# Queries, keys and values projected by three float32r products of parts, by halves of the rows

## The chip, the cores and the metric

The kernel runs on one core of one Trainium2 chip. The metric is the device time of one execution in microseconds; each given time is that of the whole program. Five engines work side by side, each with its own instruction stream in program order: TensorE (PE in the profile; PEld is its weight load), VectorE (DVE), ScalarE (ACT), GpSimd (POOL) and SyncE (SP, which here only starts transfers). They wait for one another on semaphores.

## The reference, cut to what matters

```python
x = x + attn(layernorm(x), qkv_w, qkv_b, out_w, out_b)            # x: (4, 1024, 256)
x = x + xattn(layernorm(x), ctx_1024, ...)                         # context: (4, 77, 256)
x = x + ffn(layernorm(x), W_router, b_router, W1, b1, W2, b2)      # 8 experts, top 2
# attn:
qkv = x @ qkv_w.T + qkv_b                                          # 256 -> 768, all rows
qkv = qkv.reshape(batch, seq_len, 16, 48).transpose(0, 2, 1, 3)
q, k, v = jnp.split(qkv, 3, axis=-1)                               # 16 heads of 16
scores = jnp.einsum('bhid,bhjd->bhij', q, k) / 4 + alibi_bias
out = jnp.einsum('bhij,bhjd->bhid', softmax(scores), v)
```

All is float32. The change touches the first product, from 256 features to the queries, keys and values of 1024 rows, once for each of four batches.

## The kernel before, in words

The program has three stages. In the **opening** (0 to about 90 us) batch 0 is normalized, turned and projected, and the row maxima of its first group of heads are taken. In the **attention stage** (to about 1085 us) 16 groups run, four for each batch, each of four heads. A group has 64 units; a unit is one score product of 128 keys by 512 queries (`score`, L1110), its exponential on ScalarE (`exp`, L1360), a quarter of an `attend` (L1124, products with the values), and, for a later group, one product for row maxima (`max`, L1150) with its reduction on VectorE (`maxed`, L1539; in the first group L1536 reduces two at once). In the **expert stage** (to the end) 71 blocks of 128 rows pass through the experts.

What sets the order is `plan()`. It writes one list of steps and each engine runs its own kinds of step in the order of the list. Beside the units it places side work in two lanes. The lane "next" prepares batch b+1 during batch b (`prepare`); the lane "done" completes batch b-1. `behind()` gives each lane a budget per unit (`PACE_NEXT`, `PACE_DONE`), and the number behind each `yield` is what a step takes of it. `TAKES` holds the planner's costs, by which `until()` and `room()` hold a step back until its input or its PSUM bank should be ready.

`prepare(b)` before: `layer_norm` (statistics L1579, `norm` L1378 from `xr_next` into `xn_next`), four `turn`s (L1171, four 128x128 transposes each into one of two side banks) with their copies `turned` (L1386) into `xT_next`, which holds all 1024 rows. Then 8 projections `proj` per batch: `mo` is the half of the 256 output features, `a` is queries or keys, `ch` is the half of the rows. Each is two float32 products of 512 columns (L1180), one per half `c` of the input features, and each of these two is a part of its own in the order. A projection is split into three bfloat16 parts: `high` on ScalarE (L1394), `rest` on VectorE (L1610, from PSUM into one of two buffers `rest_of`), and `mid` and `low` (L1511, L1514) on GpSimd, in the first half of batch 0 on VectorE. Last come 4 `vproj` per batch (L1189), each of two parts of two float32 products of 256 columns, and `values` (L1623) reads the result.

The parts of the queries and keys are written to DRAM (`stage`, L1013; for the first half of batch 0 `first_half`, L998 on SP, L1402 on ACT) and read back in stacked form (`spread`, L987, L988; for the first group L1001 on SP and L1352 on ACT). The first `max` waits for the stacked rows of the first group (`first_rows`).

An fp32 product is issued as two instructions in the trace, so 4 batches x 8 x 2 products are the 128 instructions of L1180.

## Time and profile before

| | us |
|---|---|
| median of 3 runs | 1623.58 |
| lowest and highest | 1622.12, 1631.59 |
| the profiled execution, its own time | 1623.51 |
| its span in the profile | 1621.7 |

```profile
PE 1563.1 (96%) x10430; PEld 952.5 (59%) x10430; DVE 1180.4 (73%) x2393; ACT 936.4 (58%) x1788; POOL 392.2 (24%) x463
PE   5999999999999999999999999989999999999996
DVE  4887877878777788886777777523444788888885
PE 89%; DVE 4%; ACT 3%; issue 2%; DMA 1%; POOL 0%; ACTq 0%; DVEq 0%; SPq 0%; POOLq 0%
```

The first line has each engine's busy time, its share of the span and its instructions. The next two show the busy share in 40 slices of 40.5 us, in tenths. The last is the chain of waits that ended last: at each step from the last instruction back, which engine the time belongs to. Matmuls overlap in the records, so a busy PE is not PE at its peak: what a product costs is read from the distance between starts, not from its duration.

### The profile page before, as it was taken

How to read it: one execution, taken by the hardware profiler on the slowest of the kernel's cores; microseconds unless marked ns; L12 is line 12 of the kernel's file. 1: busy time of each engine (PE TensorE's matmuls, PEld its weight loads, DVE VectorE, ACT ScalarE, POOL GpSimd, SP SyncE). 2: the span in 40 equal slices, each digit the busy share in tenths (PEclk: the TensorE clock that was granted, in tenths of full speed). 3: DMA queues.
4: the chain of work that ended last, by engine and by line, in shares of the span. 5: the costliest groups of instructions: out<-in, count | busy, mean ns of one | idle time of the engine just before them, and what ended most of it. 6: DMA issues, size and time to landing. Idle time of an engine off the chain costs nothing.

```text
span 1621.7 us, 30987 instructions
## 1 busy us (share of the span) xinstructions
PE 1563.1 (96%) x10430; PEld 952.5 (59%) x10430; DVE 1180.4 (73%) x2393; ACT 936.4 (58%) x1788; POOL 392.2 (24%) x463
## 2 busy tenths in 40 slices
PE   5999999999999999999999999989999999999996
PEld 2433343343444444345444344438999999999996
DVE  4887877878777788886777777523444788888885
ACT  3156656666555766754665755872222566666663
POOL 6201120001210041310013100051243433453443
PEclk9899999999999999999999999999999999999998
DMA  6663341133141440314234333134566776666663
GB/s 177 111 125 58 78 82 23 22 44 56 36 61 65 69 74 23 43 40 82 51 65 76 36 113 131 62 127 143 144 192 190 194 200 215 201 197 196 195 191 85
DMA packets 92670, 173.40 MB, mean 107 GB/s; under 512 B 13235, under 2 KB 51123, under 8 KB 92384
## 3 DMA queue, kind: packets, MB, share of 16 engines
q1 hardware_dynamic: 75376, 143.69, 35.1%
q0 software_dynamic: 15744, 26.54, 7.7%
q8 instruction: 84, 1.38, 0.4%
q10 hardware_dynamic: 1392, 1.18, 0.4%
q14 instruction: 74, 0.61, 0.1%
HBM read 133.69 MB, written 37.29 MB: 105 GB/s over the span
## 4 chain that ended last, share of the span: by engine, by line
PE 89%; DVE 4%; ACT 3%; issue 2%; DMA 1%; POOL 0%; ACTq 0%; DVEq 0%; SPq 0%; POOLq 0%
PE ps L1316 15%; PE ps L1124 15%; PE ps L1150 14%; PE ps L1110 13%; PE ps L1079 8%; PE ps L1342 4%; PE ps L1180 3%; PE ps L1202 2%; PE ps L1171 2%; PE ps L1236 2%; PE ps L1113 2%; PE ps L1153 2%; DVE rmax L1539 2%; ACT prob L1360 2%; PE ps L1189 2%
## 5 line engine op out<-in xcount | busy, mean ns | idle before, releaser
L1539 DVE TENSOR_REDUCE rmax<-ps 128x1 f32<-128x512 f32 x960 | 622.5, 684 | 187.6 <-PE ps L1150 91.2
L1360 ACT ACTIVATE prob<-ps 128x512 f32<-128x512 f32 x1024 | 559.6, 605 | 316.2 <-PE ps L1113 165.6
L1150 PE MATMUL ps<-stacked_k,stacked_q 112*128 112x512 bf16 x1024 | 389.7, 387 | 11.2 <-DMA stacked_k<-parts_of_rows 3.4
L1110 PE MATMUL ps<-stacked_q,stacked_k 115*128 115x512 bf16 x1024 | 357.4, 381 | 4.8 <-ACT prob L1360 3.2
L1124 PE MATMUL ps<-prob,values 128*32 128x512 f32 x2048 | 272.8, 605 | 5.8 <-ACT prob L1360 5.3
L1316 PE MATMUL ps<-xiT,w_now 128*128 128x128 f32 x2272 | 267.7, 276 | 1.0 <-issue 1.0
L1316 PEld LDWEIGHTS ps<-xiT,w_now 128*128 128x128 f32 x2272 | 262.5, 193 | 2.0 <-issue 1.2
L1150 PEld LDWEIGHTS ps<-stacked_k,stacked_q 112*128 112x128 bf16 x1024 | 99.1, 98 | 279.5 <-DVE rmax L1539 183.4
L1110 PEld LDWEIGHTS ps<-stacked_q,stacked_k 115*128 115x128 bf16 x1024 | 98.0, 98 | 160.5 <-ACT prob L1360 79.1
L1939 POOL DMA_INDIRECT out<-yo,xi x71 | 116.5, 1640 | 247.8 <-DVE yo L1827 240.9
L1466 ACT ACTIVATE hidT<-ps,b 128x128 f32<-128x128 f32 x284 | 80.1, 364 | 87.8 <-PE ps L1316 77.8
L1813 DVE TENSOR_TENSOR w_low<-w,w_high 128x2048 fp32r<-128x2048 f32 x51 | 116.9, 2293 | 5.5 <-issue 4.0
L1476 ACT ACTIVATE hid_high<-hidT 128x512 fp32r<-128x512 f32 x102 | 64.6, 633 | 94.3 <-DVE hidT L1796 92.6
L1079 PE MATMUL ps<-w_high,hid_high 128*128 128x256 f32 x408 | 118.7, 291 | 0.0
L1796 DVE TENSOR_SCALAR hidT<-ps,b 128x128 f32<-128x128 f32 x284 | 80.1, 344 | 47.5 <-PE ps L1316 37.9
L1079 PE MATMUL ps<-w_low,hid_high 128*128 128x256 f32 x408 | 114.6, 281 | 0.0
L1079 PE MATMUL ps<-w_high,hid_low 128*128 128x256 f32 x408 | 114.6, 281 | 0.0
L1153 PE MATMUL ps<-ramps,slopes 128*128 128x128 f16 x512 | 112.7, 220 | 0.0
L1113 PE MATMUL ps<-ramps,slopes 128*128 128x128 f16 x512 | 112.3, 219 | 0.0
L1853 POOL TENSOR_TENSOR rstd_of<-varp,minus_half 128x8 f32<-128x8 f32 (+1 forms) x14 | 20.8, 1485 | 362.9 <-DVE varp L1587 362.9
L1488 ACT ACTIVATE w_high<-w 128x2048 fp32r x51 | 97.6, 1913 | 17.7 <-issue 16.0
L1805 DVE TENSOR_TENSOR hid_low<-hidT,hid_high 128x512 fp32r<-128x512 f32 x102 | 70.2, 688 | 45.5 <-ACT hid_high L1476 45.5
(201 smaller groups left out, 1853.1 us busy)
## 6 DMA issues: line engine op xcount, KB each, us to landing
w_now<-in_w SPq DMA_DIRECT2D x71, 1024.0 KB
stacked_q<-parts_of_rows SPq DMA_DIRECT2D x90, 128.0 KB, 6.2
stacked_k<-parts_of_rows SPq DMA_DIRECT2D x90, 128.0 KB, 6.8
xi<-expert_rows SPq DMA_DIRECT2D x71, 130.0 KB
w<-in_w SPq DMA_DIRECT2D x8, 1024.0 KB
parts_of_rows<-q_part SPq DMA_DIRECT2D x21, 256.0 KB, 6.8
parts_of_rows<-k_part SPq DMA_DIRECT2D x21, 256.0 KB, 7.1
xr<-in_x POOLq DMA_DIRECT2D x4, 1024.0 KB, 9.9
```

Source lines behind the costliest of these rows:

```text
L1079: last = e.matmul(ps[:, bank, 0:D], rows[n % 2][:, c, :], weights[n % NPARTS][:, c, :], start=(c == 0 and i == 0), stop=(c == FC - 1 and i ...
L1110: m = e.matmul(ps[:, bank, :], ka[i][0:ROWS, hh, kt * P:(kt + 1) * P], qa[i][0:ROWS, hh, ch * BANK:(ch + 1) * BANK], start=True, stop=True)
L1113: m = e.matmul(ps[:, bank, (kt % 4) * P:(kt % 4 + 1) * P], slopes[:, g * HG + hh, :], ramps[:, kt % 2, :], start=False, stop=True, skip_gr ...
L1124: m = e.matmul(ps[CT * hh:CT * (hh + 1), AV_BANK, :], vt[b % 2][:, kt, c0:c0 + CT], prob[:, unit_of(G, ch, kt, hh) % NPROB, :], start=(kt ...
L1150: m = e.matmul(ps[:, bank, :], qa[i][0:MAX_ROW, hh, qt * P:(qt + 1) * P], ka[i][0:MAX_ROW, hh, kc * BANK:(kc + 1) * BANK], start=True, sto ...
L1153: m = e.matmul(ps[:, bank, (qt % 4) * P:(qt % 4 + 1) * P], slopes[:, g * HG + hh, :], ramps[:, 1 - qt % 2, :], start=False, stop=True, ski ...
L1316: m = e.matmul(ps[:, 1 + 2 * (n % 2) + half, q * P:(q + 1) * P], w1_now[n % NW][:, c, f * P:(f + 1) * P], xiT[n % 2][:, c, :], start=(c == ...
L1360: e.activation(prob[:, u % NPROB, :], ps[:, score_bank(u), :], ACT.Exp).then_inc(sem["exp"], 1)
L1488: e.activation(w2_high[n % NPARTS][:, :, :], second_layer(expert, slice(0, FC)), ACT.Copy).then_inc(sem["w2_high"], 1)
L1539: e.tensor_reduce(rmax[:, G % 2, hh * NT + qt, kc:kc + 1], ps[:, p.bank("max", *k), :], AX.X, ALU.max).then_inc(sem["maxed"], 1)
L1813: e.tensor_tensor(w2_low[n % NPARTS][:, chunks, :], second_layer(expert, chunks), w2_high[n % NPARTS][:, chunks, :].bitcast(F32), ALU.subt ...
L1939: e.indirect_dma_start(t["out"], bass.IndirectOffsetOnAxis(ap=xi[n % NX][:, TOKEN:TOKEN + 1].bitcast(I32), axis=0), yo[n % NY][:, :], None ...
```

## The change

Queries, keys and values are now sums of three products of parts. An operand is split into a float32r part `high` and a float32r part `low` (the rest). `x_turn` transposes the normalized rows into a bank; `x_high` (ScalarE) copies the bank into `xT_parts`, and `x_low` (VectorE) subtracts that from the bank. The weights are split once, in three pieces: `w_high` on ScalarE, the first piece's `w_low` on VectorE, the other two (`w_low_late`) on GpSimd. Each float32 product of 512 or 256 columns becomes high x high, high x low and low x high. The normalization writes in place in `xr_next`; `xn_next` and `xT_next` are gone. From batch 1 on one half of the rows is held in parts at a time: transposes, four projections and two value products of the first half, then those of the second. In batch 0 the first half's transposes and its first projection go ahead of the second half's transposes. `fetch_next` (GpSimd's load of the next rows) moves behind the second half's transposes, and there are three buffers `rest_of`.

```diff
+NREST = 3
...
+    def x_parts(b, c, four):
+        if c == 0 and users["next"]:
+            p.free["x_high", b, c, four] = users["next"]
+        yield from until("x_turn")
+        if b:
+            yield from room()
+        add("x_turn", b, c, four)
+        add("x_high", b, c, four)
+        empty("x_low", b, c, four)
+        yield 6
...
+    def project(b, mo, a, ch):
+        yield from until("proj")
+        yield from room()
+        yield from in_parts("proj", b, mo, a, ch)
+        add("high", b, mo, a, ch)
+        for kind in ("rest", "mid", "low"):
+            empty(kind, b, mo, a, ch)
+        yield 8
+    def project_values(b, two):
+        yield from room()
+        yield from in_parts("vproj", b, two)
+        empty("values", b, two)
+        yield 9
...
+    def prepare_first():
+        yield from layer_norm("pre", 0, WHOLE, (0, NT // 2 + 1))
+        add("scale_q")
+        add("w_high", 0)
+        add("w_low", 0)
+        yield from x_parts(0, 0, 0)
+        add("norm", "pre", 0, NT // 2 + 1)
+        yield from x_parts(0, 1, 0)
+        for tt in range(NT // 2 + 2, NT):
+            add("norm", "pre", 0, tt)
+        yield from project(0, 0, 0, 0)
+        for c in range(DC):
+            yield from x_parts(0, c, 1)
+        for i in range(1, DC + 1):
+            add("w_high", i)
+            add("w_low_late", i)
+        yield from project(0, 0, 1, 0)
+        for a in range(2):
+            yield from project(0, 0, a, 1)
+        for ch in range(NCH):
+            add("first_half", ch)
+        split.add((0, 0))
+        now["spread"] = 1
+        spread_when_ready()
+        yield 0
+        for a in range(2):
+            for ch in range(NCH):
+                yield from project(0, 1, a, ch)
+        flush()
+        yield 0
+        for two in range(NT // 2):
+            yield from project_values(0, two)
+        users["next"] = ("vproj", 0, NT // 2 - 1)
...
     def prepare(b):
         yield from layer_norm("pre", b, WHOLE)
-        if 0 < b < NB - 1:
-            add("fetch_next", b + 1)
-        yield from turn("pre", b, WHOLE)
-        if b == 0:
-            add("scale_q")
-        yield from until("proj", "pre")
-        for mo in range(DC):
-            first = (b, mo) == (0, 0)
-            for one in range(2):
-                for other in range(2):
-                    a, ch = (other, one) if first else (one, other)
-                    yield from room()
-                    yield from in_parts("proj", b, mo, a, ch)
-                    add("high", b, mo, a, ch)
-                    for kind in ("rest", "mid", "low"):
-                        empty(kind, b, mo, a, ch)
-                    yield 10
-            if first:
-                for ch in range(NCH):
-                    add("first_half", ch)
-                split.add((b, mo))
-                now["spread"] = 1
-                spread_when_ready()
-                yield 0
-            elif b:
-                staging.append(stage_out(b, mo))
-            else:
-                flush()
-                yield 0
-        for two in range(NT // 2):
...
+        for ch in range(NCH):
+            for c in range(DC):
+                yield from x_parts(b, c, ch)
+            if ch == NCH - 1 and b < NB - 1:
+                add("fetch_next", b + 1)
+            for mo in range(DC):
+                for a in range(2):
+                    yield from project(b, mo, a, ch)
+                if ch == NCH - 1:
+                    staging.append(stage_out(b, mo))
+            for two in range(2 * ch, 2 * ch + 2):
+                yield from project_values(b, two)
+            users["next"] = ("vproj", b, 2 * ch + 1)
...
-            wqkv = sb("wqkv", [P, DC, 3 * D])
+            wqkv_high, wqkv_low = (sb(f"wqkv_{n}", [P, DC, 3 * D], F32R) for n in ("high", "low"))
...
-            rest_of = [sb(f"rest_of{i}", [P, BANK]) for i in range(2)]
...
+            rest_of = [sb(f"rest_of{i}", [P, BANK]) for i in range(NREST)]
...
-            xn_next = sb("xn_next", [P, NT, D])
-            xT_next = sb("xT_next", [P, DC, S])
+            xT_parts = sb("xT_parts", [P, 2, DC, BANK], F32R)
...
-        kraw = prob[:, 0:4, :].rearrange("p a n -> p (a n)").rearrange("p (a n) -> p a n", a=2)
+        kraw = xT[:, :, :]
+        wqkv = flat(xn[:, :, :])[:, 0:DC * 3 * D].rearrange("p (c n) -> p c n", c=DC)
...
-        normed_of = lambda which: {"pre": xn_next, "on": on}.get(which, xn)
-        turned_of = lambda which: (xT, xT_next)[lane(which)]
...
+        normed_of = lambda which: {"pre": xr_next, "on": on}.get(which, xn)
...
+        first_low = flat(w2_high[0][:, :, :]).rearrange("p (h c n) -> p h c n", h=NCH, c=DC)
+        x_high_of = lambda b, ch: xT_parts[:, 0 if b else ch, :, :]
+        x_low_of = lambda b, ch: xT_parts[:, 1, :, :] if b else first_low[:, ch, :, :]
...
+                elif kind == "x_turn":
+                    b, c, four = k
+                    if (b, c, four) == (0, 0, 0):
+                        e.wait_ge(sem["proj_in"], 64)
+                    if c == 0:
+                        e.wait_ge(sem["norm"], p.upto("norm", "pre", b, 4 * four + 3))
+                    bank = side_bank(kind, *k)
+                    for q in range(4):
+                        m = e.transpose(ps[:, bank, q * P:(q + 1) * P], xr_next[:, 4 * four + q, c * P:(c + 1) * P], ident[:, :])
+                    m.then_inc(sem["x_turn"], 1)
...
-                    if (mo, a, ch) == (0, 0, 0) and first:
-                        e.wait_ge(sem["turned"], p.upto("turned", "pre", b, DC - 1, NCH - 1))
-                        if b == 0:
-                            e.wait_ge(sem["scale_q"], 1)
+                    if (mo, a) == (0, 0) and first:
+                        e.wait_ge(sem["x_low"], p.upto("x_low", b, DC - 1, ch))
+                    if b == 0 and first:
+                        if mo == 0:
+                            e.wait_ge(sem["w_low"], 1)
+                        else:
+                            e.wait_ge(sem["w_low_late"], 1)
                     bank = side_bank(kind, *k, first=first)
-                    m = e.matmul(ps[:, bank, :], wqkv[:, part, a * D + mo * P:a * D + (mo + 1) * P],
-                                 xT_next[:, part, ch * BANK:(ch + 1) * BANK], start=first, stop=final)
+                    cols = slice(a * D + mo * P, a * D + (mo + 1) * P)
+                    high, low = x_high_of(b, ch)[:, part, :], x_low_of(b, ch)[:, part, :]
+                    e.matmul(ps[:, bank, :], wqkv_high[:, part, cols], high, start=first, stop=False)
+                    e.matmul(ps[:, bank, :], wqkv_high[:, part, cols], low, start=False, stop=False)
+                    m = e.matmul(ps[:, bank, :], wqkv_low[:, part, cols], high, start=False, stop=final)
                     if final:
                         m.then_inc(sem["proj"], 1)
                 elif kind == "vproj":
                     b, two = k
+                    if b == 0 and first:
+                        e.wait_ge(sem["w_low_late"], 2)
...
+                    if b == 0 and first:
+                        e.wait_ge(sem["w_low_late"], 2)
                     bank = side_bank(kind, *k, first=first)
-                    tt = 2 * two + part
+                    tt, cols = 2 * two + part, slice(2 * D, 3 * D)
+                    rows = slice(tt % 4 * P, (tt % 4 + 1) * P)
+                    into = ps[:, bank, part * D:(part + 1) * D]
                     for c in range(DC):
-                        m = e.matmul(ps[:, bank, part * D:(part + 1) * D], xT_next[:, c, tt * P:(tt + 1) * P], wqkv[:, c, 2 * D:3 * D],
-                                     start=(c == 0), stop=(c == DC - 1))
+                        high, low = x_high_of(b, tt // 4)[:, c, rows], x_low_of(b, tt // 4)[:, c, rows]
+                        e.matmul(into, high, wqkv_high[:, c, cols], start=(c == 0), stop=False)
+                        e.matmul(into, high, wqkv_low[:, c, cols], start=False, stop=False)
+                        m = e.matmul(into, low, wqkv_high[:, c, cols], start=False, stop=(c == DC - 1))
                     if final:
                         m.then_inc(sem["vproj"], 1)
...
+                elif kind == "x_high":
+                    b, c, four = k
+                    before = p.free.get((kind, *k))
+                    if before:
+                        e.wait_ge(sem[before[0]], p.upto(*before))
+                    e.wait_ge(sem["x_turn"], p.upto("x_turn", *k))
+                    e.activation(x_high_of(b, four)[:, c, :], ps[:, p.bank("x_turn", *k), :], ACT.Copy).then_inc(sem["x_high"], 1)
+                elif kind == "w_high":
+                    i, = k
+                    e.wait_ge(sem["scale_q"], 1)
+                    e.activation(piece(wqkv_high, i), piece(wqkv, i), ACT.Copy).then_inc(sem["w_high"], 1)
...
+                elif kind == "w_low":
+                    i, = k
+                    e.wait_ge(sem["w_high"], i + 1)
+                    e.tensor_tensor(piece(wqkv_low, i), piece(wqkv, i), piece(wqkv_high, i).bitcast(F32), ALU.subtract).then_inc(sem["w_low"], 1)
+                elif kind == "x_low":
+                    b, c, four = k
+                    e.wait_ge(sem["x_high"], p.upto("x_high", *k))
+                    e.tensor_tensor(x_low_of(b, four)[:, c, :], ps[:, p.bank("x_turn", *k), :], x_high_of(b, four)[:, c, :].bitcast(F32),
+                                    ALU.subtract).then_inc(sem["x_low"], 1)
...
-                    if n > 2:
-                        e.wait_ge(sem["low"], n - 2)
-                    e.scalar_tensor_tensor(out=rest_of[n % 2][:, :], in0=ps[:, p.bank("proj", *k), :], scalar=bqk[:, a, mo:mo + 1],
+                    if n > NREST:
...
+                elif kind == "w_low_late":
+                    i, = k
+                    e.wait_ge(sem["w_high"], i + 1)
+                    e.tensor_tensor(piece(wqkv_low, i), piece(wqkv, i), piece(wqkv_high, i).bitcast(F32), ALU.subtract).then_inc(sem["w_low_late"], 1)
...
-                    e.wait_ge(sem["norm"], p.upto("norm", "pre", b - 1, NT - 1))
+                    e.wait_ge(sem["x_turn"], p.upto("x_turn", b - 1, DC - 1, NCH - 1))```

The planner's costs change with it (`proj` 0.86 to 0.65, `vproj` 0.86 to 0.7, `x_low` 0.75 and so on), and with these the places of all later steps by a few units. What the new order looks like at three places:

PE in the attention stage, batch 1, first projection; before (L1180 is a float32 product, L1150 and L1110 are maxima and scores, L1153 and L1113 their small products):

```order
L1180 MATMUL ps<-xT_next,wqkv 128x512
L1150 MATMUL ps<-stacked_k,stacked_q 128x512
L1153 MATMUL ps<-ramps,slopes 128x128
L1110 MATMUL ps<-stacked_q,stacked_k 128x512
L1113 MATMUL ps<-ramps,slopes 128x128
L1150 MATMUL ps<-stacked_k,stacked_q 128x512
L1180 MATMUL ps<-xT_next,wqkv 128x512
```

and in the change (L1250 to L1252 are the three products, L1207 and L1167 maxima and scores):

```order
L1250 MATMUL ps<-xT_parts,wqkv_high 128x512
L1251 MATMUL ps<-xT_parts,wqkv_high 128x512
L1252 MATMUL ps<-xT_parts,wqkv_low 128x512
L1207 MATMUL ps<-stacked_k,stacked_q 128x512
L1210 MATMUL ps<-ramps,slopes 128x128
L1167 MATMUL ps<-stacked_q,stacked_k 128x512
L1170 MATMUL ps<-ramps,slopes 128x128
L1207 MATMUL ps<-stacked_k,stacked_q 128x512
L1250 MATMUL ps<-xT_parts,wqkv_high 128x512
L1251 MATMUL ps<-xT_parts,wqkv_high 128x512
L1252 MATMUL ps<-xT_parts,wqkv_low 128x512
```

Each part has three instructions in the place of one float32 product; between the two parts stands the same other work.

PE in the change, batch 1, between the last transposes of the second half (L1236) and its first projection (L1181 is `attend`):

```order
L1236 MATMUL ps<-ident,xr_next 128x128 x4
L1167 MATMUL ps<-stacked_q,stacked_k 128x512
L1207 MATMUL ps<-stacked_k,stacked_q 128x512
L1210 MATMUL ps<-ramps,slopes 128x128
L1167 MATMUL ps<-stacked_q,stacked_k 128x512
L1207 MATMUL ps<-stacked_k,stacked_q 128x512
L1181 MATMUL ps<-prob,values 32x512 x4
L1207 MATMUL ps<-stacked_k,stacked_q 128x512
L1210 MATMUL ps<-ramps,slopes 128x128
L1167 MATMUL ps<-stacked_q,stacked_k 128x512
L1250 MATMUL ps<-xT_parts,wqkv_high 128x512
```

Nine rows of other work stand between them. This hand-over now comes twice per batch; before, it came once.

VectorE in the opening, from the shift of batch 0 on; before:

```order
L1593 SCALAR_TENSOR_TENSOR shift_of<-mv,rstd_of 128x8
L1597 CAST stacked_q<-prob 128x2048
L1598 CAST stacked_k<-on 16x1024
L1601 TENSOR_SCALAR wqkv<-wqkv 128x2x256
L1602 TENSOR_SCALAR bqk<-bqk 128x2
L1603 ISA
L1610 SCALAR_TENSOR_TENSOR rest_of<-ps,bqk,q_part 128x512
L1511 CAST q_part<-rest_of 128x512
L1514 TENSOR_TENSOR q_part<-rest_of,q_part 128x512
L1610 SCALAR_TENSOR_TENSOR rest_of<-ps,bqk,k_part 128x512
```

and in the change (L1689, L1690 scale the query weights, L1695 is `w_low`, L1699 `x_low`, L1685, L1686 the casts of the position rows, L1707, L1599, L1602 are `rest`, `mid`, `low`):

```order
L1681 SCALAR_TENSOR_TENSOR shift_of<-mv,rstd_of 128x8
L1689 TENSOR_SCALAR xn<-xn 128x2x256
L1690 TENSOR_SCALAR bqk<-bqk 128x2
L1691 ISA
L1695 TENSOR_TENSOR wqkv_low<-xn,wqkv_high 128x2x2x128
L1699 TENSOR_TENSOR w_high<-ps,xT_parts 128x512 x2
L1685 CAST stacked_q<-xT 128x2048
L1686 CAST stacked_k<-on 16x1024
L1707 SCALAR_TENSOR_TENSOR rest_of<-ps,bqk,q_part 128x512
L1599 CAST q_part<-rest_of 128x512
L1602 TENSOR_TENSOR q_part<-rest_of,q_part 128x512
L1699 TENSOR_TENSOR w_high<-ps,xT_parts 128x512 x2
```

The scaling and the first splits stand ahead of the casts, and the second half's two `x_low` stand between the first query part and the first key part.

## Rows read from the trace of the kernel before

**Rows 1.** Busy time by stage: stretch, its length, each engine's busy time, clock, DMA.

```profile
35.00:58.00 23.00, 20.33 (x89) 10.90 (x90) 21.89 (x27) 1.37 (x2) 13.24 (x17) 0.98 0.58 140
58.00:66.00 8.00, 6.94 (x14) 0.79 (x12) 7.81 (x7) 0.00 (x0) 0.00 (x0) 0.50 0.89 141
...
92.00:160.00 68.00, 65.59 (x398) 24.09 (x397) 57.21 (x116) 46.06 (x89) 6.14 (x6) 1.00 0.50 100
160.00:1085.00 925.00, 913.17 (x5634) 392.97 (x5631) 699.85 (x1408) 595.33 (x1125) 139.10 (x157) 1.00 0.31 63
```

**Rows 2.** The chain of waits by line: first 92 to 160 us, then 92 to 1085.

```profile
by line: PE ps L1150 22.1%; PE ps L1124 20.6%; DVE rmax L1539 17.3%; PE ps L1110 15.2%; PE ps L1180 5.9%; DVE stats_of L1579 3.9%; PE ps L1113 3.3%; PE ps L1153 2.6%; PE ps L1171 2.6%; issue 1.9%; ACT prob L1360 1.8%; PE ps L1132 1.5%; DVE 
...
by line: PE ps L1124 24.4%; PE ps L1150 21.9%; PE ps L1110 21.2%; PE ps L1180 4.3%; PE ps L1113 2.7%; PE ps L1153 2.6%; ACT prob L1360 2.6%; PE ps L1202 2.6%; DVE rmax L1539 2.3%; PE ps L1236 2.2%; PE ps L1189 2.2%; PE ps L1171 2.1%; issue 
```

**Rows 3.** Groups by line, 92 to 1085 us: the instructions of batches 1 to 3.

```profile
L1180 PE MATMUL ps<-xT_next,wqkv 128*128 128x512 f32 x96 | 50.5, 608 | 0.5 <-ACT xT_next L1386 0.5
...
L1189 PE MATMUL ps<-wqkv,xT_next 128*128 128x256 f32 x96 | 25.2, 385 | 0.0
```

**Rows 4.** Timeline of PE: start, duration; a projection part among other products.

```profile
168.42 1.06 PE L1124 MATMUL ps<-prob,values 128*32 128x512 f32 x8
...
169.92 0.38 PE L1150 MATMUL ps<-stacked_k,stacked_q 112*128 112x512 bf16 x1
170.14 0.38 PE L1110 MATMUL ps<-stacked_q,stacked_k 115*128 115x512 bf16 x1
170.36 1.02 PE L1180 MATMUL ps<-xT_next,wqkv 128*128 128x512 f32 x2
171.22 0.38 PE L1150 MATMUL ps<-stacked_k,stacked_q 112*128 112x512 bf16 x1
```

**Rows 5.** Timeline of PE: a part of a value product.

```profile
237.27 1.03 PE L1189 MATMUL ps<-wqkv,xT_next 128*128 128x256 f32 x4
238.13 0.38 PE L1150 MATMUL ps<-stacked_k,stacked_q 112*128 112x512 bf16 x1
```

**Rows 6.** Timeline of PE, expert stage: a block's first float32r products, 256 columns.

```profile
1534.39 0.36 PE L1079 MATMUL ps<-w_high,hid_high 128*128 128x256 f32 x1
1534.59 0.28 PE L1079 MATMUL ps<-w_low,hid_high 128*128 128x256 f32 x1
1534.71 0.28 PE L1079 MATMUL ps<-w_high,hid_low 128*128 128x256 f32 x1
```

**Rows 7.** Durations in ns (least/median/most) of like operations, from their tiles and lines.

```profile
L1386 ACT ACTIVATE xT_next<-ps x16: 575/597/632, 14.6 to 643.3; 128x512 f32<-128x512 f32 x16
...
L1476 ACT ACTIVATE hid_high<-hidT x102: 631/633/636, 1266.4 to 1602.9; 128x512 fp32r<-128x512 f32 x102
...
L1635 DVE TENSOR_TENSOR xr<-ps,xr x32: 678/680/692, 342.4 to 1164.7; 128x512 f32<-128x512 f32 x32
...
L1514 POOL TENSOR_TENSOR q_part<-rest_of,q_part x14: 1151/1157/1163, 35.4 to 715.8; 128x512 bf16<-128x512 f32 x14
```

**Rows 8.** Timeline of the opening, all engines.

```profile
12.86 1.09 PE L1171 MATMUL ps<-ident,xn_next 128*128 128x128 f32 x4 [12.86 <-ACT xn_next L1378]
...
15.18 1.23 DVE L1597 CAST stacked_q<-prob 128x2048 bf16<-128x2048 f32 x1 [4.57 <-DMA sc<-in_c_slopes]
...
18.34 13.24 PE L1180 MATMUL ps<-xT_next,wqkv 128*128 128x512 f32 x24 [0.69 <-ACT xT_next L1386]
...
26.29 0.73 DVE L1514 TENSOR_TENSOR k_part<-rest_of,k_part 128x512 bf16<-128x512 f32 x1
...
28.81 2.82 ACTq L1352 DMA_DIRECT2D stacked_k<-parts_of_rows  x6
...
34.71 0.61 POOL L1511 CAST q_part<-rest_of 128x512 bf16<-128x512 f32 x1 [7.21 <-DVE rest_of L1610]
...
34.95 0.39 PE L1150 MATMUL ps<-stacked_k,stacked_q 112*128 112x512 bf16 x1 [3.38 <-DMA stacked_k<-parts_of_rows]
```

**Rows 9.** DMA issues: KB each, us from issue to landing.

```profile
bv_all<-in_bv SPq DMA_DIRECT2D x1, 128.0 KB, 7.5
```

55 lines of the change are left out of this document (30 added, 25 removed).

## The prediction

> **What bounds the kernel now.** I read the busy times by stage first, then the chain of waits, then the timeline of one projection and of the opening. Only batch 0's projections lie in the opening; those of batches 1 to 3 stand between the scores of the attention stage, so the question is what that stage waits for. From 160 to 1085 us PE is busy 913 of 925 us, VectorE 700, ScalarE 595 and GpSimd 139 [rows 1]. In the chain over 92 to 1085 us every large entry is a product on PE; VectorE's maxima hold 2.3% and ScalarE's exponentials 2.6% [rows 2]. Ahead of the projections' 96 instructions PE sat idle 0.5 us in all [rows 3]. So PE is the bound there, and what a product gives back on PE mostly comes off the end. The exception is 92 to 160 us, where maxima and statistics together hold 21% of the chain [rows 2] and VectorE is busy 57 of 68 us [rows 1]. In the opening VectorE is the bound from the first maxima on: 21.9 of 23 us from 35 to 58 us [rows 1]. What comes ahead of them is one chain from the first transposes to the landing of the stacked keys [rows 8].
>
> **Projections, batches 1 to 3.** The distance between starts is the price. The part of a projection at 170.36 us is followed at 171.22, so a float32 product of 512 columns takes 0.86 us [rows 4]. In its place come three float32r products. No row has one of 512 columns. The nearest are a bfloat16 product of 512 columns, 0.22 us (169.92 to 170.14) [rows 4], and float32r products of 256 columns, 0.12 us apart (1534.59 to 1534.71), so 0.24 for twice the columns [rows 6]. I take 0.22, since the distance there has a fixed share that does not double: 3 x 0.22 = 0.66, saved 0.20. The 96 instructions are 48 such parts [rows 3]: 48 x 0.20 = 9.6 us, with 0.24 only 48 x 0.14 = 6.7.
>
> **Value products, batches 1 to 3.** A part (two float32 products of 256 columns) takes 0.86 us (237.27 to 238.13) [rows 5]. Six float32r products at 0.12 take 0.72, by the row of just this shape [rows 6]. The 96 instructions are 24 parts [rows 3]: 24 x 0.14 = 3.4 us. Each product brings its own weight load; in the expert stage each has one too and the distance is still 0.12, so I add nothing for it. The first of such a run is 0.20 ahead of the second (1534.39 to 1534.59) [rows 6], 0.08 more; if each part pays that, it takes 24 x 0.08 = 1.9 us here and 48 x 0.08 = 3.8 of the projections' gain.
>
> Sum on PE 13.0 us, at the other end 13.0 - 2.9 - 1.9 - 3.8 = 4.4. The trace's 0.12 is a little above the gap that the Trainium skill gives in "TensorE: Matmul & The Clock Gate", Back-to-back issue gap (262 cycles at 256 columns, 518 at 512: 0.109 and 0.216 us). By those figures the sum would be, as an estimate, 48 x 0.21 + 24 x 0.20 = 15 us; the measured 0.12 decides for 256 columns.
>
> Of the 13.0 us about 94% lies on the chain, since maxima and exponentials hold 5 to 6% of it [rows 2]: -12.2 us.
>
> **What it adds in that stage.** Transposes and ScalarE's copies keep their number, 12 each, and `x_high` is a copy like the old one, 0.60 us [rows 7]. New are 12 `x_low` on VectorE, priced by an addition of the same size that also reads PSUM, 0.68 us [rows 7]: 8.2 us of VectorE time over 925 us in which it has 225 free. It costs at VectorE's share of the chain: 2.3% of most and 21% of the two that fall before 160 us, 0.4 us. A side bank is now held for copy and subtraction instead of the copy, 0.7 us longer, 12 times; the other bank and the scores cover it, except in part: +0.4. The hand-over transposes, `x_high`, `x_low`, projection takes 0.60 + 0.68 and a queued maximum of about 0.68, some 2 us; between the last transposes and the projection PE has one `attend` of at most 1.06 us and six products of 0.22 [rows 4], 2.4 us. It is covered in the middle of the estimate and short by up to 2 us where VectorE's queue is longer. Six of these halves: +0.7 here, 0 to 12 as ends, the upper for the rival below. GpSimd's later `fetch_next` has over 100 us until its rows are read; a third `rest_of` can only remove a wait. Both nothing. In sum +1.5.
>
> **The opening.** Before, the four transposes, their four copies and the casts end ahead of the projection at 18.34 us [rows 8]. Now it needs half the rows. Transposes can start at 12.86 as before [rows 8]. The last of the first four loads that it waits for is issued at about 4.3 and takes 7.5 [rows 9], so it is there at 11.8, and the weights are scaled, two short operations, by about 13.2 at the latest (the transposes stood ready at 12.86). `w_high`, 0.63 by the like copy [rows 7], ends at about 13.9; `x_high` for c=0 at 14.5; then one `norm` and `x_high` for c=1 by about 15.7; `x_low` at 16.5. The projection starts 1.8 us earlier. It does not all arrive: the position rows' casts, 1.23 us the larger, began at 15.18 [rows 8] and now end near 18.6, 1.4 later, with SP's writes behind them; and two `x_low` of the second half, 1.4 us, are ahead of the first key part on VectorE. Its `low` ended at 27.02 [rows 8]; I get about 26. The keys' loads (28.81) and the first maximum (34.95) [rows 8] follow it, so -0.9. GpSimd has been idle 7.21 us before 34.71 [rows 8], so its two late `w_low`, 1.16 each by the like subtraction [rows 7], hide there; without that cover they would push the next projections by 2.3. In 35 to 58 us VectorE is short of full by 1.1 us [rows 1]; faster products give back perhaps 0.4. Sum -1.3. Ends: -2.9 if the casts and splits cost nothing, +1.5 if SP's later writes are what the stacked rows then wait for.
>
> The clock is one reason for a spread. From 58 to 66 us the granted clock is 0.50 [rows 1], the lower level of 1.2 GHz, after a stretch in which PE had only sparse maxima. Shorter products leave it more gaps; VectorE's 7.8 of 8 us there cover a slow PE [rows 1], so it is worth 1 us at most.
>
> **Sum.** -12.2 + 1.5 - 1.3 = -12.0. Against the profiled execution's 1623.51 us, which is 0.07 below the median of 1623.58: **1611.5 us**. The forecast's own ends: 1623.5 - 13.0 + 0.4 - 2.9 = 1608, about 1606 with luck in the order, and 1623.5 - 4.4 + 3 + 1.5 = 1623.6; the worst ends will not all meet, and I take 1621.
>
> **Rivals.**
> *More than the sum.* The new order and the planner's smaller costs also close gaps: maxima and exponentials hold about 5% of 993 us in the chain [rows 2], 49 us, and if a sixth of that goes, 8 us more: 1604. For it: side work leaves each unit sooner and PE's waits shift with every order. Against: PE has 12 of 925 us free between its records [rows 1], and gaps of other causes stay. 22%. By the Trainium skill's gaps, named above, the estimate would be 2 us nearer to this one.
> *The gain is lost in hand-overs.* `x_low` stands in VectorE's in-order queue behind maxima, and PE, in order too, stops at the first product until it is through. Six halves at 2 us are 12 us: 1623.5. For it: two engines now follow each other ahead of each half. Against: 2.4 us of other work and VectorE's 24% idle [rows 1]. 13%.
> *Slower: a float32r product of 512 columns runs at half rate.* Then it costs what one of the two instructions of a float32 product costs, 0.43 us, three cost 1.29 against 0.86, and 48 parts lose 20.6 us, those of the opening some 3 more; with the value products' -3.4 and +1.5 that is 1623.5 + 21.7 = 1645. It decides from 0.30 us a product on. For it: no row shows the shape. Against: at 256 columns the rate is full [rows 6]. 5%.
> That the change does not do what it says is left out: the order has three products in the place of one everywhere.
>
> **Chances.** The forecast itself 60%, the rivals 22, 13 and 5. About 1% (16 us) is what a measurement of this kernel can tell from no change. Faster by over 1% means below 1607.3: most of the first rival and a little of the forecast's lower end, 0.29. Slower is the half-rate rival and a bit of the hand-overs, 0.06. The rest, 0.65, is within 1%, most of it on the faster side. A range of 1603 to 1621 takes in the first rival and the forecast's ends.
>
> **What the changed kernel's profile would show.** Starts of L1250 to L1252 0.22 apart (0.43: half rate), of L1265 to L1267 0.12. PE's busy time from 92 us to the experts shorter by some 13 us, VectorE's longer by 8. PE's waits for `x_low` ahead of L1250 under 1 us each; several of 2 us would be the lost gain. The first L1207 near 34 us. Wrong would make it: a chain with VectorE above 10% after 160 us, or an expert stage of another length than now, which nothing here touches.

## The result and the profile after

| | median us | runs | ratio to before, 95% interval |
|---|---|---|---|
| before | 1631.31 (1619.92 to 1634.32) | 15 | |
| changed | 1619.53 (1614.59 to 1632.22) | 15 | 0.995 (0.9926 to 0.9973) |

The medians are 11.8 us apart; the ratio goes by the means (1628.7 and 1620.5) and puts the gain at 0.5%, 8 us. The changed kernel takes 8 us more than the forecast of 1611.5. The three times shown of before were mostly low ones: its 15 runs fall into 1620 to 1624 us (five) and 1631 to 1634 us (ten), and 1623.58 belongs to the lower group. What parts the groups is the granted clock (last of the experiments).

Busy times by stage, of the changed kernel's profiled execution (1626.87 us, span 1625.1), in the columns of [rows 1]:

```profile
92.00:160.00 68.00, 65.02 (x396) 24.64 (x400) 60.17 (x119) 44.95 (x86) 5.50 (x6) 1.00 0.44 85
...
160.00:1078.00 918.00, 906.00 (x5744) 399.66 (x5737) 708.69 (x1421) 599.77 (x1130) 143.08 (x162) 1.00 0.32 65
```

PE still sets the pace from 160 us on: 906 of 918 us. VectorE has some 9 us more there than in [rows 1] and 3 us more from 92 to 160, with the new `x_low`. The first and the last exponentials of the attention stage (timeline of ScalarE; before first, the changed kernel below it) give the length of that stage:

```profile
90.95 3.86 ACT L1360 ACTIVATE prob<-ps 128x512 f32<-128x512 f32 x7 [2.58 <-PE ps L1113]
...
1079.52 4.27 ACT L1360 ACTIVATE prob<-ps 128x512 f32<-128x512 f32 x8 [0.35 <-PE ps L1113]
```

```profile
92.84 2.72 ACT L1437 ACTIVATE prob<-ps 128x512 f32<-128x512 f32 x5 [2.58 <-PE ps L1170]
...
1071.80 4.27 ACT L1437 ACTIVATE prob<-ps 128x512 f32<-128x512 f32 x8 [0.35 <-PE ps L1170]
```

From the first start to the last end it is 992.8 us before and 983.2 after: 9.6 us less. But the stage begins 1.9 us later, and from its last exponential to the end of the span the changed kernel needs 549.0 us, before 537.9. These 1.9 and 11.1 us are what ate the gain in this execution, which at 1626.87 us is the second slowest of its 15.

In one place of the stage the granted clock (third column from the right) fell, which in this execution of before it did not between 92 and 1085 us:

```profile
540.00:550.00 10.00, 9.81 (x71) 5.80 (x70) 5.62 (x12) 3.53 (x7) 0.00 (x0) 0.88 0.94 164
550.00:560.00 10.00, 10.00 (x60) 3.20 (x56) 8.10 (x30) 6.57 (x14) 0.00 (x0) 0.95 0.01 2
```

That is 1.7 us of lost clock; without it the stage would be 11.3 us shorter than before.

A projection part and a value part in PE's timeline, to set beside [rows 4] and [rows 5]:

```profile
162.24 0.38 PE L1207 MATMUL ps<-stacked_k,stacked_q 112*128 112x512 bf16 x1
162.27 0.58 PE L1250 MATMUL ps<-xT_parts,wqkv_high 128*128 128x512 f32 x1
162.69 0.39 PE L1251 MATMUL ps<-xT_parts,wqkv_high 128*128 128x512 f32 x1
162.92 0.40 PE L1252 MATMUL ps<-xT_parts,wqkv_low 128*128 128x512 f32 x1
163.16 0.39 PE L1207 MATMUL ps<-stacked_k,stacked_q 112*128 112x512 bf16 x1
...
170.51 0.38 PE L1207 MATMUL ps<-stacked_k,stacked_q 112*128 112x512 bf16 x1
...
171.43 0.39 PE L1207 MATMUL ps<-stacked_k,stacked_q 112*128 112x512 bf16 x1
```

The two later products stand 0.23 and 0.24 us apart. The whole part takes 163.16 - 162.24 = 0.92 with one 0.22 us product ahead, so 0.70; forecast 0.66. The value part takes 171.43 - 170.51 - 0.22 = 0.70; forecast 0.72. The half-rate rival is dead.

The opening of the changed kernel (timeline, to set beside [rows 8]):

```profile
10.17 2.00 POOL L1954 MEMSET values<- 128x2296 f32 x1
11.57 2.82 DVE L1689 TENSOR_SCALAR xn<-xn 128x512 f32<-128x512 f32 x1 [1.17 <-DMA bv_all<-in_bv]
12.11 2.00 POOL L1955 MEMSET values<- 128x2296 f32 x1
...
17.29 1.27 DVE L1685 CAST stacked_q<-xT 128x2048 bf16<-128x2048 f32 x1
...
25.69 0.73 DVE L1602 TENSOR_TENSOR k_part<-rest_of,k_part 128x512 bf16<-128x512 f32 x1
25.92 1.45 SPq L1055 DMA_DIRECT2D parts_of_rows<-k_part  x3
27.44 2.69 POOL L1966 TENSOR_TENSOR wqkv_low<-xn,wqkv_high 128x512 fp32r<-128x512 f32 x2
27.61 1.37 DVE L1599 CAST q_part<-rest_of 128x512 bf16<-128x512 f32 x1
28.85 1.37 ACTq L1429 DMA_DIRECT2D stacked_k<-parts_of_rows  x3
29.02 1.66 DVE L1602 TENSOR_TENSOR q_part<-rest_of,q_part 128x512 bf16<-128x512 f32 x1
...
35.42 0.39 PE L1207 MATMUL ps<-stacked_k,stacked_q 112*128 112x512 bf16 x1 [2.31 <-DMA stacked_k<-parts_of_rows]
```

The scaling of the query weights (L1689) took 2.82 us. In the kernel before the same operation took 0.41:

```profile
12.32 2.00 POOL L1858 MEMSET values<- 128x2296 f32 x1
...
17.13 0.41 DVE L1601 TENSOR_SCALAR wqkv<-wqkv 128x512 f32<-128x512 f32 x1
...
25.32 2.06 SPq L998 DMA_DIRECT2D parts_of_rows<-k_part  x3
```

In the changed kernel it ended at 14.39, when GpSimd's second memset had ended. The memsets stood in the same place before; what moved is the scaling, from behind them into them. The projection began at 17.43, 0.9 earlier than before; the forecast had 1.8. The position rows' casts began at 17.29 instead of 15.18. VectorE was through with the first key part at 26.42, 0.6 earlier than before ([rows 8]), but SP, whose earlier transfers wait for those casts, wrote it out until 27.37, before until 27.38. So the keys' loads stayed (28.85 against 28.81), 1.5 us behind that in both. The first maximum came at 35.42 instead of 34.95.

Then the expert stage. From block `FINE` (20) on an expert's second weights are split as well (`w_high` on ScalarE, `w_low` on VectorE) and multiplied as float32r parts. The scatters are GpSimd's writes of the rows to where the blocks read them (`expert_rows`); `xiT` holds a block's turned rows and `yo` its output. Timeline of the changed kernel about the first of these splits, with PE's waits, then the busy times:

```profile
1253.31 1.91 ACT L1576 ACTIVATE w_high<-w 128x2048 fp32r x1 [9.62 <-DMA expert_rows<-xn,slot]
1255.36 2.29 DVE L1910 TENSOR_TENSOR w_low<-w,w_high 128x2048 fp32r<-128x2048 f32 x1 [8.05 <-ACT w_high L1576]
...
1256.58 5.47 PE L1393 MATMUL ps<-xiT,w_now 128*128 128x128 f32 x32 [2.61 <-ACT xiT L1540]
1265.05 5.11 PE L1419 MATMUL ps<-w,hidT 128*128 x16 [2.79 <-DVE yo L1924]
```

```profile
1240.00:1260.00 20.00, 17.39 (x116) 16.21 (x115) 7.58 (x25) 7.01 (x14) 5.18 (x5) 0.94 0.68 195
1260.00:1280.00 20.00, 15.82 (x106) 14.58 (x105) 14.21 (x44) 6.17 (x13) 4.24 (x6) 0.89 0.54 160
```

Before, in the same two stretches:

```profile
1240.00:1260.00 20.00, 20.00 (x143) 18.97 (x143) 11.86 (x40) 6.30 (x16) 6.21 (x5) 1.00 0.62 177
1260.00:1280.00 20.00, 19.70 (x146) 18.66 (x146) 15.62 (x40) 11.04 (x18) 8.94 (x6) 1.00 0.61 166
```

ScalarE stood 9.62 us at `w_high` of block 20, until batch 3's last scatter of rows had landed. Behind it in ScalarE's queue were the copies `xiT` that PE waits for, and behind VectorE's `w_low` the sum `yo`. PE lost 6.8 of 40 us, and the clock fell (0.94 and 0.89).

### The profile page after: what moved, and what is told of

Same layout as the page of the kernel before. It is cut to its first block, busy times and chain, and to the rows that moved or that the text cites. A ratio compares the mean times of both kernels' runs of the same rounds, so it can differ in the third digit from the quotient of the medians.

```text
span 1625.1 us, 31278 instructions
## 1 busy us (share of the span) xinstructions
PE 1554.7 (96%) x10558; PEld 965.7 (59%) x10558; DVE 1197.9 (74%) x2410; ACT 940.4 (58%) x1791; POOL 385.1 (24%) x465
## 4 chain that ended last, share of the span: by engine, by line
PE 85%; DVE 5%; DMA 3%; ACT 3%; issue 2%; SPq 0%; DVEq 0%; ACTq 0%; POOL 0%; POOLq 0%
PE ps L1181 15%; PE ps L1207 14%; PE ps L1393 14%; PE ps L1167 13%; PE ps L1136 8%; PE ps L1419 3%; DMA out<-yo,xi 2%; PE ps L1279 2%; PE ps L1313 2%; PE ps L1210 2%; PE ps L1170 2%; DVE rmax L1627 2%; ACT prob L1437 1%; PE ps L1226 1%; PE ps L1294 1%
## 5 line engine op out<-in xcount | busy, mean ns | idle before, releaser
L1627 DVE TENSOR_REDUCE rmax<-ps 128x1 f32<-128x512 f32 x960 | 621.1, 685 | 176.5 <-PE ps L1210 86.2
L1437 ACT ACTIVATE prob<-ps 128x512 f32<-128x512 f32 x1024 | 560.9, 601 | 308.2 <-PE ps L1167 156.0
L1207 PE MATMUL ps<-stacked_k,stacked_q 112*128 112x512 bf16 x1024 | 391.1, 389 | 12.6 <-DVE rmax L1624 5.1
L1167 PE MATMUL ps<-stacked_q,stacked_k 115*128 115x512 bf16 x1024 | 358.6, 381 | 3.0 <-ACT prob L1437 1.6
L1181 PE MATMUL ps<-prob,values 128*32 128x512 f32 x2048 | 273.6, 606 | 6.8 <-ACT prob L1437 6.8
L1393 PE MATMUL ps<-xiT,w_now 128*128 128x128 f32 x2272 | 269.7, 277 | 7.1 <-ACT xiT L1540 4.2
L1393 PEld LDWEIGHTS ps<-xiT,w_now 128*128 128x128 f32 x2272 | 263.9, 193 | 9.9 <-ACT xiT L1540 5.0
L1207 PEld LDWEIGHTS ps<-stacked_k,stacked_q 112*128 112x128 bf16 x1024 | 99.4, 99 | 280.0 <-DVE rmax L1627 182.7
L1167 PEld LDWEIGHTS ps<-stacked_q,stacked_k 115*128 115x128 bf16 x1024 | 97.7, 98 | 151.1 <-ACT prob L1437 68.8
L1910 DVE TENSOR_TENSOR w_low<-w,w_high 128x2048 fp32r<-128x2048 f32 x51 | 117.0, 2293 | 13.5 <-ACT w_high L1576 8.0
L1576 ACT ACTIVATE w_high<-w 128x2048 fp32r x51 | 97.6, 1914 | 27.2 <-issue 13.8
L1210 PE MATMUL ps<-ramps,slopes 128*128 128x128 f16 x512 | 113.2, 221 | 0.0
L1170 PE MATMUL ps<-ramps,slopes 128*128 128x128 f16 x512 | 112.5, 220 | 0.0
L2006 POOL DMA_INDIRECT expert_rows<-xn,slot x64 | 62.2, 971 | 160.9 <-ACT prob L1437 126.7
## 6 DMA issues: line engine op xcount, KB each, us to landing
stacked_q<-parts_of_rows SPq DMA_DIRECT2D x90, 128.0 KB, 6.3
stacked_k<-parts_of_rows SPq DMA_DIRECT2D x90, 128.0 KB, 6.9
```

The source lines that it names most:

```text
L1167: m = e.matmul(ps[:, bank, :], ka[i][0:ROWS, hh, kt * P:(kt + 1) * P], qa[i][0:ROWS, hh, ch * BANK:(ch + 1) * BANK], start=True, stop=True)
L1170: m = e.matmul(ps[:, bank, (kt % 4) * P:(kt % 4 + 1) * P], slopes[:, g * HG + hh, :], ramps[:, kt % 2, :], start=False, stop=True, skip_gr ...
L1181: m = e.matmul(ps[CT * hh:CT * (hh + 1), AV_BANK, :], vt[b % 2][:, kt, c0:c0 + CT], prob[:, unit_of(G, ch, kt, hh) % NPROB, :], start=(kt ...
L1207: m = e.matmul(ps[:, bank, :], qa[i][0:MAX_ROW, hh, qt * P:(qt + 1) * P], ka[i][0:MAX_ROW, hh, kc * BANK:(kc + 1) * BANK], start=True, sto ...
L1210: m = e.matmul(ps[:, bank, (qt % 4) * P:(qt % 4 + 1) * P], slopes[:, g * HG + hh, :], ramps[:, 1 - qt % 2, :], start=False, stop=True, ski ...
L1393: m = e.matmul(ps[:, 1 + 2 * (n % 2) + half, q * P:(q + 1) * P], w1_now[n % NW][:, c, f * P:(f + 1) * P], xiT[n % 2][:, c, :], start=(c == ...
```

## The experiments

To compare kernels whose clock differs I use a worked-out number beside the median: the span times the mean granted clock of the same run, averaged over the runs. At a grant of 0.5 half the time is lost, so the product is about the time at the full clock. (It also counts stretches that VectorE covers, such as 58 to 66 us, but these are in every kernel.) "Stage" is the start of the first exponential to the start of the last, "rest" what follows it in the profiled execution; the figure in brackets is the same stretch times its own granted clock, summed over stretches of 10 us. The first profile of before has 992.3 (992.3) and 538.5 (530.9).

The runs of before timed beside these were in three groups: 1607.0 +- 0.5 beside the two repeats and the two FINE = 22 kernels that follow first, 1606.5 +- 0.6 beside after_oldnumbers, before_numbers, fill_late_fine22 and x_low_twice_fine22, 1606.2 +- 0.8 beside the last four run. So differences of 0.8 us between groups mean nothing.

| kernel | median us | span x clock, +- 2 s.e. | stage | rest |
|---|---|---|---|---|
| before_again | 1631.94 | 1607.0 +- 1.0 | 992.2 (992.2) | 537.7 (530.7) |
| before_fine22 | 1627.17 | 1606.6 +- 0.8 | 998.3 (991.5) | 539.0 (530.2) |
| before_numbers | 1629.72 | 1607.8 +- 0.5 | 996.7 (989.9) | 541.7 (534.5) |
| the changed kernel | 1619.53 | 1599.3 +- 1.1 | 982.7 (981.0) | 549.6 (538.3) |
| after_again | 1620.75 | 1599.8 +- 1.1 | 982.8 (981.1) | 542.2 (534.5) |
| after_fine22 | 1613.40 | 1594.8 +- 0.8 | 982.9 (981.2) | 535.5 (529.3) |
| after_oldnumbers | 1614.48 | 1596.3 +- 0.5 | 982.4 (980.7) | 539.3 (531.7) |
| fill_late_fine22 | 1613.49 | 1593.5 +- 2.1 | 984.7 (981.3) | 536.3 (531.1) |
| fill_wait_fine22 | 1611.21 | 1592.6 +- 1.4 | 983.1 (981.4) | 538.3 (532.1) |
| best | 1615.54 | 1594.4 +- 1.6 | 983.9 (980.5) | 540.0 (531.0) |
| x_low_twice_fine22 | 1620.12 | 1599.1 +- 1.0 | 989.5 (986.1) | 535.0 (529.2) |
| x_low_none_fine22 | 1612.74 | 1594.0 +- 0.6 | 983.0 (981.3) | 534.6 (528.9) |
| two_products_fine22 | 1602.11 | 1584.6 +- 0.8 | 972.7 (971.0) | 534.9 (529.0) |

**The loss at block 20.** Four runs together: both kernels again, and both with the fine blocks from 22 on, so that the first split comes two blocks later.

```diff
-FINE = 20
+FINE = 22
```

> The changed kernel once more, for a second profiled execution. Theory: the opening is about 2 us longer than before (first score at about 92.8 us against 91.0), the attention stage about 10.5 us shorter, and what is left is lost in the expert stage, at block 20, whose weight split waits for the last batch's scatters. So again: first score at 92 to 93.5 us, end of attention at 1070 to 1073 us from the span's start, ratio to before 0.993 to 0.998. Rival, chance alone: the expert stage of the first profile (547 us from the end of attention) was a slow execution; then this one shows 536 us and no wait near block 20.

> The kernel before once more, timed against itself. Ratio 1.000 within 0.002 by every theory. Its runs so far lie at 1620 to 1624 us (5 of 15) and 1630 to 1634 us (10 of 15). Theory: the two groups differ at block 20 of the expert stage, where the last scatters land just in time (36 us of stage before 1260 us show no wait in the profile of 1623.5 us); a profile of a run near 1631 shows waits of some 8 us between 1240 and 1280 us. Rival: the difference lies elsewhere (a lower granted clock or the opening).

> The changed kernel with FINE 22 in the place of 20: the blocks 20 and 21 use the float32 product of the second layer, so the first weight split that waits for the last scatters comes two blocks, some 14 us, later. Costs 2 x 0.6 us (3.45 against 2.84 us a block). Theory: takes the waits away: median 1612 to 1615 us, ratio to before 0.988 to 0.991, and the runs lie closer together. Rival, chance alone or another cause: 1.2 us slower than the changed kernel, ratio 0.995 to 0.997.

> The kernel before with FINE 22. Theory: its slow group of runs (1630 to 1634 us) goes, since that group comes from the same wait: median 1622 to 1625 us, ratio 0.994 to 0.997. Rival: the slow group has another cause; then it stays and the median is 1632 us, ratio 1.000 to 1.001.

after_again (1620.75 us, ratio 0.995) has the wait again, a smaller one:

```profile
1248.18 1.91 ACT L1576 ACTIVATE w_high<-w 128x2048 fp32r x1 [3.49 <-DMA expert_rows<-xn,slot]
```

PE then waits 4.0 us, where the first profile has 7.0, and the granted clock stays at 1.00 there. So the collision is no accident of one execution, but its size is. before_again repeats before (ratio 0.9998). after_fine22 took 1613.40 us (ratio 0.9893, 0.9859 to 0.9927), 6 to 7 below the changed kernel. Its stretch over the same place:

```profile
1240.00:1260.00 20.00, 20.00 (x137) 18.76 (x137) 13.33 (x56) 6.48 (x16) 5.73 (x4) 1.00 0.58 158
1260.00:1280.00 20.00, 20.00 (x150) 19.17 (x149) 13.03 (x27) 10.29 (x20) 4.07 (x6) 1.00 0.81 237
```

So the loss was there. It isn't that FINE = 22 is faster by itself: in the kernel before the same edit changes the span times clock from 1607.0 to 1606.6. What was wrong was the idea that before's upper group came from this place too: before_fine22 still has runs at 1632 to 1635 us.

Why does the changed kernel collide and before not? The change also lowers the planner's numbers. With them the plan puts batch 3's last scatter behind block 16's down product (its second layer) instead of 15's, while `w_high` of block 20 stays right behind block 17's: one block lies between where there were two. The two halves of that, apart:

```diff
-"proj": 0.65, "vproj": 0.7,          PARTS = {"proj": (DC, 8), "vproj": (2, 9), ...
+"proj": 0.86, "vproj": 0.86,         PARTS = {"proj": (DC, 10), "vproj": (2, 11), ...
```

> The changed kernel with the planner's numbers of before (proj and vproj 0.86 in TAKES, PARTS (DC, 10) and (2, 11)); the products, the parts in two float32r pieces, the halves and the opening stay changed. The plan then puts batch 3's last scatter behind block 15's down product again and table 1 ends three blocks' halves earlier against the first weight split of the fine blocks. Theory (the expert stage lost 6 to 11 us because the new numbers move batch 3's end one expert block later against the switch at block 20): no wait of over 0.5 us on PE between 1230 and 1300 us, time 1612 to 1616, 4 to 7 below the changed kernel. Rival (the products themselves end the attention stage earlier, and the collision at block 20 comes from that whatever the order): waits remain, time 1618 to 1622. Second question: with shorter products but numbers that say 0.86, the attention stage should keep its end near 1076 (the saving is PE time, not order); if it ends past 1079, part of the saving was order.

> The kernel before with the planner's numbers of the change alone (proj 0.65, vproj 0.7, PARTS (DC, 8) and (2, 9), the yields 8 and 9); products stay float32. Its plan has the order of the changed kernel around the expert blocks 0 to 24. Theory: nothing is gained in the attention stage (last exponential at 1083 or later, at most 2 us away from before), and the expert stage loses what it lost in the changed kernel, with waits at blocks 19 to 21 between 1260 and 1290 us: 3 to 8 us over before, 1632 to 1638. Rival (only with shorter products does the order collide): within 2 us of before, 1625 to 1633.

after_oldnumbers keeps the changed products and has before's order there: 1614.48 us (0.9909, 0.9879 to 0.994), and its stage is as short as the changed kernel's (982.4). ScalarE's first split waits 1 us instead of 9.6 or 3.5, and PE still waits 0.9 us for `yo`, so the collision is small rather than gone, as was expected:

```profile
1245.92 1.91 ACT L1576 ACTIVATE w_high<-w 128x2048 fp32r x1 [0.97 <-DMA expert_rows<-xn,slot]
```

So the numbers cost the changed kernel some 3 us at the full clock (1599.5 to 1596.3) and gave its attention stage nothing that the products had not given. before_numbers (1629.72 us, ratio 0.9998) met only a part of what was expected: its rest is 4 us longer (PE 18.32 and 17.35 of 20 us busy from 1260 to 1300), but its stage is some 2 us shorter at the full clock (989.9), which nobody expected, so that span times clock rises by 1.3 us (1607.8 against 1606.5 beside it), little more than the errors. Its median isn't higher, since its clock was (0.9878 against 0.9872). The order alone opens the collision; what it costs varies, 4.0 and 7.0 us of waits on PE in two executions of the changed kernel.

**The price of the products.** The third product of a projection part left out in batches 1 to 3 (the weights' low part times the rows' high part is then missing):

```diff
-                    e.matmul(ps[:, bank, :], wqkv_high[:, part, cols], low, start=False, stop=False)
-                    m = e.matmul(ps[:, bank, :], wqkv_low[:, part, cols], high, start=False, stop=final)
+                    m = e.matmul(ps[:, bank, :], wqkv_high[:, part, cols], low, start=False, stop=final and b > 0)
+                    if b == 0:
+                        m = e.matmul(ps[:, bank, :], wqkv_low[:, part, cols], high, start=False, stop=final)
```

> The changed kernel with the fine blocks from 22 on, and in batches 1 to 3 a part of a projection has two products: the one of the weights' low part with the rows' high part is left out (computed less, on purpose for its price). 48 products fall away at the measured distance of 0.235 us, 11.3 us of PE. Theory (PE sets the pace of the attention stage, 94% of it on the chain): the time from the first exponential to the last falls by 10 to 11.5 us against 982.9, the span times the granted clock by 10 to 11 from 1594.8 to about 1584, the median to 1602 to 1605. Rival (other engines take over part of the path, as with x_low): less than 8 us.

Both came out: the stage 982.9 to 972.7 (at the full clock 981.2 to 971.0), span times clock 1594.8 to 1584.6, each -10.2 for 11.3 us of PE. So about 90% of what a product frees comes off the end; with the 0.8 us between the groups it could be 83%.

**The hand-over.** `x_low` of batches 1 to 3 executed twice, and not at all (then the rows' low part isn't computed):

```diff
+                    if b:
+                        then(e.tensor_tensor(x_low_of(b, four)[:, c, :], ps[:, p.bank("x_turn", *k), :],
+                                             x_high_of(b, four)[:, c, :].bitcast(F32), ALU.subtract))
```
```diff
+                    if b:
+                        e.engine_nop().then_inc(sem["x_low"], 1)
+                        continue
```

> The changed kernel with the fine blocks from 22 on, and in batches 1 to 3 each x_low on VectorE is executed twice, the second behind the end of the first: 12 x 0.75 = 9 us more of VectorE, and the hand-over ahead of each half 0.75 to 1.5 us longer. Theory (the hand-over is covered by other work of PE and VectorE has room): at most +1.5 us on 1613.4, last exponential at most 1 us later than 1076.1. Rival (hand-overs are on the path, 2 us each of six halves): +5 to +9 us, with waits of PE for x_low ahead of the first projection of a half.

> The changed kernel with the fine blocks from 22 on, and no x_low in batches 1 to 3: VectorE only waits for x_high and signals, the products read an old tile in its place (the low part of the rows isn't computed). It takes 8.2 us off VectorE and 0.7 us or more off each hand-over. Doubling x_low cost 4.3 us of span times granted clock (1594.8 to 1599.1). Theory A (x_low costs the path in proportion, also the first time): 3 to 4.5 us less, 1590.5 to 1592 of span times clock. Theory B (the first x_low is covered, only a longer hand-over shows, as the prediction's +1.5 has it): 0.5 to 2 us less, 1593 to 1594.3.

Without `x_low` the span times clock falls by 0.8 us, as much as that of before fell between the two groups, and the stage by nothing (981.3 at the full clock, 981.2 with it): one `x_low` costs nothing that can be measured, and the forecast's +1.5 was too high. Twice costs 4.3 (4.9 in the stage), 6.7 in the median, where at most 1.5 was expected, and 5 to 9 by the rival: there the cover seems used up. The start of each half's copies against the first exponential slips by 0.6 to 1.0 us a half. PE's waits by line show only a part of it, and the one for `x_low` that the rival named is small:

```profile
PE ps L1207 <- DVE rmax L1627: 3.9, 13, 0.4
...
PE ps L1189 <- DVE xT_parts L1702: 0.4, 2, 0.2
```

The first was 2.5 us in 9 waits with one `x_low`. The remaining 3 us are not placed, so how the second `x_low` reaches PE is open.

**The opening.** `add("fill")`, GpSimd's two memsets of the value tiles, moved from ahead of `specials` to behind the late weight differences, and in a second kernel with a wait besides:

```diff
         for i in range(1, DC + 1):
             add("w_high", i)
             add("w_low_late", i)
+        add("fill")
...
-    add("fill")
     add("specials")
...
                 elif kind == "fill":
+                    e.wait_ge(sem["low"], 4)
                     e.memset(vt[0][:, :, :], 1.0)
```

> The changed kernel with the fine blocks from 22 on, and with GpSimd's memsets of the step fill moved behind the late weight differences. Theory (VectorE's scaling of the weights took 2.8 instead of 0.4 us because those memsets ran on GpSimd beside it): the scaling takes about 0.4 us, the first maximum begins 1.4 to 2 us earlier (33.5 to 34.1 instead of 35.4), the first score near 91.5, the time 1611 to 1612.5, 1 to 2.5 below the same kernel with fill where it was (1613.4). Rival (the later opening was only the order of the steps): scaling again over 2 us, or the first maximum stays at 35.4, and the time stays at 1613 to 1614.

> As the run with fill behind the late weight differences, and GpSimd's two memsets also wait until VectorE has split the first half (its fourth low). There they stood beside VectorE's cast of the second key part, which took 2.94 us instead of 0.43. Theory (a VectorE copy or scaling within SBUF stands still beside a GpSimd memset, a maximum that reads PSUM doesn't): the scaling 0.43 us, the cast of the second key part 0.43 us, first maximum near 34 as with fill late, VectorE's maxima still 0.6 to 0.7 us each beside the memsets; span times clock 0 to 2 us below that run's 1593.5. Rival: GpSimd's later mid and low hold up the second output half's splits, and span times clock is 1594 to 1597.

In fill_late_fine22 the scaling took 0.43 us and the first maximum began at 34.21 instead of 35.83, but the time, expected at 1611 to 1612.5, was 1613.49 us, that of after_fine22, and the first exponential came at 94.72, later than there (93.23). From 35 to 58 us the granted clock was 0.85 in this execution. The order of causes in the opening is borne out: with the scaling short the casts began at 16.34 instead of 18.17, SP had written the first key part out at 26.47 instead of 28.21, and the keys' loads were issued at 27.93 instead of 29.68. But now the memsets stood beside the cast of the second key part:

```profile
29.16 2.01 POOL L1954 MEMSET values<- 128x2296 f32 x1
...
30.46 2.94 DVE L1599 CAST k_part<-rest_of 128x512 bf16<-128x512 f32 x1
```

With the wait they stand beside operations that read PSUM:

```profile
11.67 0.43 DVE L1689 TENSOR_SCALAR xn<-xn 128x512 f32<-128x512 f32 x1 [1.05 <-DMA bv_all<-in_bv]
...
31.53 2.01 POOL L1955 MEMSET values<- 128x2296 f32 x1 [0.61 <-DVE k_part L1602]
33.24 0.75 DVE L1707 SCALAR_TENSOR_TENSOR rest_of<-ps,bqk,q_part 128x512 f32<-128x512 f32 x1 [1.77 <-ACT q_part L1482]
33.48 2.02 POOL L1956 MEMSET values<- 128x2296 f32 x1
33.77 0.39 PE L1207 MATMUL ps<-stacked_k,stacked_q 112*128 112x512 bf16 x1
```

The first maximum came at 33.77, the first exponential at 90.1 (93.2 in after_fine22), the median was 1611.21 us (ratio 0.9881, 0.986 to 0.9903). It is the fastest version found that computes everything, but the gain over after_fine22 isn't shown: 2.2 us in span times clock, 1.4 when each is set against its own before, with errors of about 1.5. The short scaling and cast are shown, what they are worth at the end is not.

> The three findings together: the changed kernel with the planner's numbers of before, the fine blocks from 22 on and the memsets late with their wait. With the old numbers batch 3 ends one expert block earlier, which was worth 3 us with the fine blocks from 20 on; with 22 that collision is gone already, so no more than 1 us comes from them here. Expected 1610 to 1613, span times clock 1592 to 1595; rival: the gains add (1590 or less, 1606 to 1609).

best was no better: 1615.54 us. Its span times clock is as expected, its clock was lower: like after_oldnumbers it shows a drop between 1030 and 1040 us (to 0.76, there 0.85) that after_fine22 and fill_wait_fine22 don't have. Its first maximum came at 35.59, though its opening is meant to be that of fill_wait_fine22 (33.77): in both, twelve products stand ahead of that maximum behind a wait of PE for the late weight differences; they began at 29.55 there and at 31.14 here.

**Before's two groups.** before_fine22's profiled execution fell in the upper group. Up to the first weight split of the expert stage its program is that of before. The granted clock is the third column from the right, first in the kernel before, then there:

```profile
554.00:556.00 2.00, 2.00 (x16) 0.57 (x14) 1.86 (x5) 1.09 (x2) 0.00 (x0) 1.00 0.93 97
...
1040.00:1050.00 10.00, 9.62 (x74) 4.03 (x74) 7.28 (x40) 7.90 (x18) 0.17 (x1) 1.00 0.30 110
```

```profile
554.00:556.00 2.00, 2.00 (x14) 2.00 (x13) 0.91 (x2) 0.50 (x1) 0.00 (x0) 0.63 1.06 121
556.00:558.00 2.00, 2.00 (x9) 1.27 (x10) 0.62 (x1) 0.09 (x1) 0.00 (x0) 0.50 0.70 79
...
1040.00:1050.00 10.00, 10.00 (x60) 6.32 (x62) 3.15 (x15) 3.83 (x8) 0.00 (x0) 0.66 0.00 0
```

The grant falls to 1.2 GHz (0.50) for some 7 us from 555 on, although PE was busy throughout the 10 us ahead, and again between 1040 and 1050. Each costs 3.4 us, together 6.8 of the 8.6 us between the two spans. Over all 23 runs of before timed with the second set, the clock was 0.991 or 0.992 in eight (1620 to 1625 us), 0.987 in one (1629) and 0.984 or 0.985 in fourteen (1631 to 1636).

## Why the prediction was off

- **Attention stage: right.** Forecast -12.2 + 1.5 = -10.7, measured -9.6 (two executions of each kernel: 992.3 and 992.2 against 982.7 and 982.8, start to start), and -11.2 at the full clock, since both executions of the changed kernel lose 1.7 us of clock about 550 and those of before don't. Projections give 48 x (0.86 - 0.70) = 7.7 and value parts 24 x (0.86 - 0.70) = 3.8; 90% of 11.5 is 10.4, and the last 0.8 us aren't placed. Three sizes were off and nearly cancel: the term for the projections (9.6) stood on 0.22 us a product, which takes 0.235, near the other end of [rows 6], so hardly any share was seen "that does not double"; about 90%, not 94%, arrives; and the +1.5 for `x_low` and its hand-over is nothing measurable.
- **The opening: wrong in sign as far as it can be told.** "Sum -1.3" counted two short operations for the scaling and let them end at 13.2; they ended at 14.5, beside memsets into which the change had moved them. The 0.6 us that VectorE still gained on the first key part didn't arrive: SP, kept back by the later casts, wrote it out at the same time as before. That is the reason that the forecast gave for its upper end, "if SP's later writes are what the stacked rows then wait for". The late `w_low` on GpSimd began at 27.44, behind the key part, so it isn't the cause; but it did not "hide" either: VectorE's next splits took 1.37 and 1.66 us beside it, against 0.53 and 0.73 a part earlier, and PE waited 1.30 us for it. Three profiles have before's opening and six the changed one: the first maximum comes at 34.95 to 35.18 and at 34.93 to 36.17, 0.6 us later in the mean, the first exponential at 90.95 to 92.98 and at 91.07 to 93.79, 0.7 later in the mean, which is less than the spread. So the 1.9 us between the first two profiles are in part chance; that the forecast's gain is missing is sure.
- **The failed step: "an expert stage of another length than now, which nothing here touches".** It was listed among what would make the prediction wrong, and had no price and no rival. The planner's numbers touch it. At the full clock it cost 3 to 5 us (1599.5 against 1596.3 and 1594.8).
- **The clock** was put at 1 us at most. The changed kernel's runs have 0.988 in the mean, and the sum was made against an execution at 0.991; that is some 4 us. A part goes with the collision (after_fine22 and after_oldnumbers have 0.989 and 0.990), but after_again's profile has the waits and a clock of 1.00 beside them. Why the rest fell isn't known.
- **The sample of before.** 1623.58 belongs to the lower of two groups; the median of 15 is 1631.3. That the medians lie 11.8 us apart, almost the forecast's 12.0, is luck: at the full clock the gain is 7.5 us (1607.0 to 1599.5), and the rest comes from the low clock of before's upper group.
- **Sum.** At the full clock -12.0 was forecast and -7.5 measured. The stage gave 0.5 more, the opening's 1.3 didn't come, and block 20 took 3.2 to 4.7. With the clock's 4 us this is about the 8 us between 1611.5 and 1619.5. after_fine22, without the collision, took 1613.4.
- **The rivals.** More than the sum: no, the stage gave at most 0.8 us beyond its products. Lost in hand-overs: no as it was put, PE has no wait for `x_low` after the opening, and without `x_low` nothing is won; a gain was lost, but at another place. Slower at half rate: no.

## What to carry to other kernels

When an order comes from a planner, a change of its costs is a change of every place that the order sets: compare the two orders to the end of the program, and look where a queue that many wait for (here ScalarE's) gets a wait on something slow such as a landing scatter. A step moved ahead can land beside another engine's work that stops it: price VectorE's copies within SBUF beside what GpSimd does at the new place, not alone, and follow what stands behind them (here SP's queue). And take more than three runs before a forecast leans on 8 us; the mean granted clock of each run tells at once which of two groups it is in.

## What the runs showed of the hardware

- A VectorE operation that reads and writes SBUF alone stood still beside GpSimd's memsets and subtractions: scaling 0.41 to 2.82 us (3.88 in after_fine22), a cast 0.43 to 2.94 beside memsets and 0.43 to 1.37 beside a subtraction, a subtraction of two SBUF tiles 0.69 to 1.66 beside a subtraction. Beside GpSimd's row of 16 short scalings (128x128, 10.84 us in all, from 16.66 on in before) the same scaling took its 0.41. One that reads PSUM kept its 0.75 us beside the memsets (33.24 above). The Trainium skill's page "SBUF — State Buffer", section Who interferes with whom, has this as an exclusive lock on the port pair that VectorE and GpSimd share; the waits of 1 to 3 us beside the long instructions agree.
- A float32r product of 512 columns: 0.23 to 0.24 us from start to start among its like, each with its own weight load.
- The granted clock fell at the same few places (545 to 560, 1020 to 1050, 1080 to 1110 us) in some executions of a kernel and not in others. At the first two PE was busy ahead of it; at the third it was not always (1.67, 1.28, 1.19 and 0.72 of 2 us from 1090 to 1098 in before_fine22). Why it falls is open.
